# Two PSUM banks for the scores in place of three, and two for the context, in a fused attention and feed-forward layer

## What is computed

```python
s = attention(xn)          # 32 heads of 16, keys and values shared by groups of 4 heads (8 groups), causal
scores = einsum('bhqd,bhkd->bhqk', q, k); weights = softmax(masked scores / 4); ctx = weights @ v
s = ctx @ Wo + bo
g = silu(ffn(xn))          # gate and up of 512 -> 1376, silu(gate) * up, down of 1376 -> 512, each with a rank 16 addition
```

## Time and profile before

| | us |
|---|---|
| median of 3 runs | 947.27 (938.77 to 950.02) |
| profiled execution | 946.66 |
| its span | 944.9 |
| TensorE busy (share of the span) | 896.9 (95%) |
| VectorE busy | 583.7 (62%) |
| ScalarE busy | 488.5 (52%) |
| GpSimd busy | 314.7 (33%) |

### The profile page before, as it was taken

One profiled execution on the slowest core, in us unless ns is written; L12 is line 12 of the kernel. 1 busy time (PEld: TensorE's weight loads), 2 busy tenths in 40 slices (PEclk: granted clock), 3 DMA queues, 4 the chain that ended last, 5 costly groups with the idle time before them and its releaser, 6 DMA issues.

```text
span 944.9 us, 21107 instructions
## 1 busy us (share of the span) xinstructions
PE 896.9 (95%) x8075; PEld 633.1 (67%) x8075; DVE 583.7 (62%) x1688; ACT 488.5 (52%) x990; POOL 314.7 (33%) x316
## 2 busy tenths in 40 slices
PE   3898999999999999999999999999889999999997
PEld 3765667676766666667676766554667777777885
DVE  7756666666666666665656565777666666650136
ACT  3522656565555656565656565656445454546211
POOL 4231235252525343525252434441121313121133
PEclk9978999999999999999999999998999999999999
DMA  9466343333333342424242434347565647415774
GB/s 290 165 193 192 92 129 97 122 97 114 108 115 110 97 130 83 137 71 148 58 138 84 126 99 121 100 142 204 155 183 156 171 124 194 137 53 171 205 216 142
DMA packets 142946, 129.20 MB, mean 137 GB/s; under 512 B 36176, under 2 KB 104368, under 8 KB 142624
## 3 DMA queue, kind: packets, MB, share of 16 engines
q1 hardware_dynamic: 142848, 127.87, 45.6%
HBM read 74.07 MB, written 53.22 MB: 135 GB/s over the span
## 4 chain that ended last, share of the span: by engine, by line
PE 88%; DVE 5%; DMA 3%; ACT 2%; issue 2%; SPq 1%; DVEq 0%
PE bank L1011 27%; PE o L1182 14%; PE bank L1045 12%; PE s L1146 10%; PE st L1165 8%; PE bank L286 4%; PE bank L287 4%; PE bank L288 4%; DMA ring<-in_L_attn_x 2%; PE bank L986 1%; PE bank L990 1%; DMA q<-scratch_q 1%; DVE junk L1723 1%; PE s L1153 1%; ACT prob L1442 1%
## 5 line engine op out<-in xcount | busy, mean ns | idle before, releaser
L1442 ACT ACTIVATE prob<-st 128x512 f32<-128x512 f32 (+1 forms) x640 | 323.2, 554 | 263.4 <-PE st L1165 262.8
L1723 DVE CUSTOM_DVE_ANT_0 junk<-s,mask 128x128 bf16<-128x128 f32 (+3 forms) x512 | 229.1, 487 | 69.7 <-PE s L1146 67.9
L1726 DVE TENSOR_REDUCE part_max<-s 128x1 f32<-128x512 f32 x256 | 164.0, 682 | 116.3 <-PE s L1146 116.1
L1146 PE MATMUL s<-k,q 64*128 64x512 f32 (+3 forms) x768 | 150.7, 379 | 12.2 <-DVE part_max L1723 4.6
L567 POOL TENSOR_SCALAR_AFFINE_SELECT prob<-prob 128x512 f32<-128x512 f32 x128 | 81.8, 652 | 225.8 <-ACT prob L1442 224.3
L1011 PE MATMUL bank<-x_hi,w_hi 64*128 64x512 f32 (+1 forms) x704 | 150.2, 412 | 2.4 <-DVE hid L1564 1.1
L1182 PE MATMUL o<-prob,v 128*32 128x512 f32 (+3 forms) x1536 | 145.4, 497 | 0.0
L1011 PE MATMUL bank<-x_lo,w_hi 64*128 64x512 f32 (+1 forms) x704 | 142.8, 391 | 0.0
L1011 PE MATMUL bank<-x_hi,w_lo 64*128 64x512 f32 (+1 forms) x704 | 142.1, 389 | 0.0
L1165 PE MATMUL st<-q,k 64*128 64x512 f32 (+3 forms) x768 | 130.7, 356 | 2.3 <-ACT prob L1442 1.8
L1146 PEld LDWEIGHTS s<-k,q 64*128 64x128 f32 x768 | 79.1, 188 | 53.6 <-DVE part_max L1723 24.4
(11 more groups left out here) (148 smaller groups left out, 1089.0 us busy)
## 6 DMA issues: line engine op xcount, KB each, us to landing
late_context_hid_in<-scratch_hid SPq DMA_DIRECT2D x16, 1408.0 KB, 7.2
q<-scratch_q SPq DMA_DIRECT2D x60, 200.0 KB
scratch_hid<-tanh_hid_hi SPq DMA_DIRECT2D x40, 256.0 KB, 2.1
scratch_hid<-hid_lo SPq DMA_DIRECT2D x40, 256.0 KB, 2.4
scratch_o<-o_sb SPq DMA_DIRECT2D x32, 256.0 KB
scratch_q<-proj_hi SPq DMA_DIRECT2D x30, 256.0 KB
k<-scratch_k SPq DMA_DIRECT2D x30, 192.0 KB
x_again<-in_L_attn_x SPq DMA_DIRECT2D x16, 256.0 KB, 4.4
```

The source lines that it names most:

```text
L1146: pe.matmul(sb_[(p + odd) % S_BANKS][:, 0:wd], q[half, g % 2, h // 2, qt * P:(qt + 1) * P], k[half, g % 2, k0:k0 + wd], start=True, stop=T ...
L1442: nc.scalar.activation(prob[:, job % 3, h, 0:JOB_COLS[j]], st[at % ST_BANKS][:, 0:JOB_COLS[j]], ACT.Exp, scale=float(HD) ** -0.5).then_inc ...
L1723: ins = dve.tensor_tensor_reduce(junk[:, n % S_BANKS, 0:wd], bank_[:, 0:wd], mask[:, C - wd:C], 1.0, LOWEST, ALU.add, ALU.max, part[:, h, ...
L1726: ins = dve.tensor_reduce(part[:, h, qt, dst:dst + 1], bank_[:, 0:wd], AX.X, ALU.max)
```

## The change

The scores get two banks (`S_BANKS`), the context two (`ob[0]` for the lower half of the queries, `ob[1]` for the upper). The context matmuls of job 9 move from slot 2 to slot 6, ahead of those of the next group's job 0 in one set; after the last group they stay at slot 2. The wait of job 0 and job 3 for the copy of the context is now for the copy of the same half of the group before. The steps of the upper half behind job 9 move four slots later, and LAST_SLOTS grows from 18 to 22.

```diff
--- before.py
+++ after.py
@@ -51,7 +51,8 @@
 MASKED = [j for j in range(NJ) if DIAGONAL[j]]
 SLOTS = NJ * REP
 
-TOGETHER = {0: [0], 2: [1, 2], 4: [3, 4], 6: [5, 6], 8: [7, 8], 9: [9]}
+
+TOGETHER = {0: [-1, 0], 2: [1, 2], 4: [3, 4], 6: [5, 6], 8: [7, 8]}
 
 
 
@@ -65,7 +66,7 @@
 
 
 
-S_BANKS, ST_BANKS = 3, 2
+S_BANKS, ST_BANKS = 2, 2
 TURN_BEHIND = NU_A + 7
 STREAM = []
 for _g in range(N):
@@ -85,12 +86,12 @@
 
 EVEN_SLOTS = range(22, 31)
 CONTEXT = 2
-COPY_O = [15, 3]
-STORE_O = [16, 4]
-LOAD_SUMS = [24, 10]
-INVERT = [29, 14]
-STORE_INV = [31, 16]
-LAST_SLOTS = 18
+COPY_O = [15, 7]
+STORE_O = [16, 8]
+LOAD_SUMS = [24, 14]
+INVERT = [29, 18]
+STORE_INV = [31, 20]
+LAST_SLOTS = 22
 
 
 
@@ -388,7 +389,7 @@
 
         sb_ = [psum(f"s{i}") for i in range(S_BANKS)]
         st = [psum(f"st{i}") for i in range(ST_BANKS)]
-        ob = psum("o")
+        ob = [psum(f"o{a}") for a in range(2)]
         bank = [psum(f"bank{i}") for i in range(2)]
 
 
@@ -486,7 +487,7 @@
         raw_weights = (gate_w, up_w)
 
         def bank_of(key):
-            return (*bank, *sb_, *st, ob)[BANKS[key][0]]
+            return (*bank, *sb_, *st, *ob)[BANKS[key][0]]
 
         def wait_filled(engine, key):
             engine.wait_ge(filled, NUMBER[key] + 1)
@@ -1175,11 +1176,11 @@
                     pe.wait_ge(exp_done, REP * (job + 1))
                 if j == 0:
                     pe.wait_ge(v_loaded[i % 3], DMA * (i // 3 + 1))
-                if JOBS[j][0][0] == 0 and job > 0:
-                    pe.wait_ge(o_copied, 2 * i + HALF[j])
+                if JOBS[j][0][0] == 0 and i > 0:
+                    pe.wait_ge(o_copied, 2 * (i - 1) + HALF[j] + 1)
                 for kt, q0, q1, col in JOBS[j]:
                     for h in range(REP):
-                        mm = pe.matmul(ob[32 * h:32 * h + 2 * HD, q0 % C:q0 % C + q1 - q0],
+                        mm = pe.matmul(ob[HALF[j]][32 * h:32 * h + 2 * HD, q0 % C:q0 % C + q1 - q0],
                                        v[:, i % 3, kt].rearrange("p a e -> p (a e)"),
                                        prob[:, job % 3, h, col:col + q1 - q0],
                                        start=kt == 0, stop=j in HALF_END)
@@ -1198,8 +1199,9 @@
                     j, h = divmod(n, REP)
                     last = NJ * i + j - 1
                     if h == CONTEXT and 0 <= last < NJ * N:
-                        for back in TOGETHER.get(last % NJ, []):
-                            context(last - last % NJ + back)
+                        for back in [NJ - 1] if last == NJ * N - 1 else TOGETHER.get(last % NJ, []):
+                            if last - last % NJ + back >= 0:
+                                context(last - last % NJ + back)
                     yield
 
             interleave(attention(), background())
@@ -1456,7 +1458,7 @@
                     act.wait_ge(o_stored[a], DMA * g)
                 else:
                     act.wait_ge(ones_put, 4 * DMA)
-                nc.scalar.activation(o_sb[:, a], ob[:, :], ACT.Copy).then_inc(o_copied, 1)
+                nc.scalar.activation(o_sb[:, a], ob[a][:, :], ACT.Copy).then_inc(o_copied, 1)
 
             def attention():
                 for i, n in rounds():
```

## The result

The changed kernel takes 1057.8 us (median; 1057.6 to 1065.1), the kernel before 945.5 us (938.8 to 950.0 in the runs beside it). The ratio is 1.1215, 95% interval 1.1166 to 1.1265: slower. The forecast was 1055 us, range 1015 to 1078. The profiled execution took 1057.64 us.

A forecast was written before the change was run, and what follows sets the result against it. TensorE, busy 48.54 of 48.70 us a round, was taken as the bound. Profiled 946.7 us plus 117 for score-bank waits, minus 5.6 for merged context sets, minus 3 for small credits, gave 1055 us; range 1015 to 1078.

The forecast's parts named there:

- The pairs: Score matmul pairs on TensorE must wait for both earlier VectorE reads: 4.8 us a steady round, 74 us in all.
- The turns: Turns of the maxima wait for VectorE's read of the score issued just ahead: 3.2 us a round, 43 in all.
- The sum of a round: Pairs and turns together add 7.9 us to a steady round of 48.7 us, which then lasts some 56.
- The merge: Job 9's context matmuls join the set at slot 6: 0.35 to 0.37 us saved, 15 times, 5.6 us in all.
- The second context bank, the moved copies: Two context banks gain 0; the upper half's copies and DMAs, four slots later, cost 0 to 5 us, taken as 0.
- the small credit of 3 us: Existing TensorE waits shrink where a new stall stands just ahead: 3 us off, bounds 0 and 15.
- Only the turns cost: Rival: pairs in a row recover between them, their 74 us shrink to little, 984 us; chance 0.14, including down to halfway.
- The stall spreads to ScalarE: Rival: late turns delay ScalarE's copy and exponential, 0.5 us at each of 31 turns, 1070 us; chance 0.10 with above.
- The waits fit in: Rival: pairs need 38 us of a 48.7 us round, so no wait binds, 941 us; chance 0.04, wholly or nearly.
- The rule on PSUM: Skill page: tiling speeds TensorE but not the emptying of PSUM; as a rate alone, the round gets no longer, 941 us.
- the loss of overlap: Own waits in the kernel before: a pair's two matmuls starting apart lose 0.23 us; if equally weighty, within 3 us of before.
- my two cases: Own waits in the kernel before: earlier first scores give 5 to 10 us less, or lost overlap leaves it within 3.

## Why the prediction was right

*The pairs.* The prediction subtracted, place by place, and had 4.8 us a round; the difference of the rounds with and without them is 4.9. For single places these lines of the kernel before are needed too:

```profile
395.30 0.42 PE L1011 MATMUL bank<-x_lo,w_hi 64*128 64x512 f32 x2
...
396.75 0.30 PE L1165 MATMUL st<-q,k 64*128 64x256 f32 x2
...
409.96 0.29 PE L1146 MATMUL s<-k,q 64*128 64x256 f32 x2
```

Slot 9's pair is 444.97 - (444.05 + 0.23) = 0.69 us behind its usual step, of which 0.22 was there before (395.75, where 0.23 behind the matmul at 395.30 is 395.53), so 0.47 as predicted. Slot 10's pair stands 446.94 - 445.98 = 0.96 us behind the matmul ahead of it, where it stood 397.10 - 396.75 = 0.35, so 0.61, predicted 0.60. That the delays may be added up, because VectorE is released by TensorE and moves with it, is what made the sum come out: in the changed kernel VectorE sits idle for 0.59 and 0.65 us before its reads at slots 8 and 9, waiting for TensorE.

*The turns.* Predicted 1.53 us at slot 6 and 1.65 at slot 22, 3.2 in all. In the changed kernel the turn of slot 6 moved from 0.20 to 1.76 us behind its pair, 1.56. That of slot 22 moved from 410.19 - 409.96 = 0.23 to 462.64 - 460.75 = 1.89, 1.66:

```profile
460.75 0.38 PE L1147 MATMUL s<-k,q 64*128 64x256 f32 x2
462.64 0.27 PE L1154 MATMUL s<-ident,neg_pad 128*32 128x128 f32 x1 [1.50 <-DVE part_max L1725]
```

The runs with the turn elsewhere put both at 3.0 us a round, 0.2 less than predicted. In the total they put the turns at 46 us against 43 and the pairs at 71 against 74; single runs of one kernel lie up to 7 us apart there, so the totals neither confirm nor correct that split.

*The sum of a round.* 48.7 + 7.9 - 0.4 = 56.2 us is what the prediction comes to (it says "some 56"), and 56.31 is measured.

*The merge.* 0.35 to 0.37 us a round was predicted from the entry, the exit and the start of a set, and 56.66 - 56.31 = 0.35 is measured.

*The second context bank, the moved copies.* Taken at nothing; the rounds with one and two context banks (56.65, 56.66) agree.

*The term that no run bears out* is the small credit of 3 us for waits that would be absorbed. In the steady rounds no absorption shows: they are 7.55 us longer, and 7.9 less the merge's 0.37 is 7.5. In the whole run it can't be settled. The profiled execution is 1057.6 us, and 946.7 + 117 - 5.6 without the credit is 1058.1. But executions of the kernel before lie between 938.8 and 950.0, those of the changed kernel between 1057.6 and 1065.1, and the late rounds of the changed kernel hold 75 us at a granted clock of 0.84, where the kernel before has 60 us at 0.89 (640 to 700 us); the prediction has no term for that. That the total comes out within 3 us is therefore in part luck; the agreement of the rounds and of the single places is not.

*The rivals.* Only the turns cost (984 us): refuted by the kernel with the turn apart, where the pairs alone make it 1018. The stall spreads to ScalarE (1070 us): TensorE's waits for exponentials are 1.9 us in all after the change, 1.8 before. The waits fit in (941 us): VectorE was busy for 56% of the span and yet TensorE waited for it 159 times, so what counts is not its rate.

*The rule on PSUM.* The Trainium skill's page "TensorEngine Tiling (Array Packing)", section "Performance Considerations", names the emptying of PSUM as the possible limit. Taken as a rate it gave 941 us, and the measurement decides against that. As a statement on where to look it holds: in the run with half the columns the length of the reads moves the time by 73 us.

## What to carry to other kernels

A bank in a ring is worth what it lets the consumer do *behind* the producer's back: list for each user of the ring which read it waits for with n and with n - 1 banks, and subtract the start from that read's end in the trace of the kernel as it is. Look above all for odd users of the ring (here the turn): one fewer bank can make them wait for work issued just ahead of them. And where two instructions go out as a pair, give each its own wait; in the kernel before, that alone took 1.5% off.

## What the runs showed of the hardware

Two matmuls in different row halves of the array need not run in step. With a wait on the second alone, the first and its successors go on at 0.23 us a pair while the second half follows some 0.2 us behind (the 0.61 us rows above), and in the kernel before with own waits the stagger is gone 1.7 us later (the 0.39 us row at 341.17). This holds for waits up to about the length of one matmul: where the second waited for longer, in the changed kernel with own waits, the next pair started only 0.46 us behind. I had given the loss of overlap a case of its own; in the kernel before, the round got 0.95 us shorter, where 5 to 10 us in the total (0.3 to 0.6 a round) was the better of my two cases.
